# A graph network of four layers on one core: the tiles for further edges of the relation layer, one ahead of the other

## What is computed

```
agg  = segment_sum(x[src], edge_type * n + dst)          # 34 relations x 625 nodes
mean = agg / max(count, 1)
h1   = einsum('nri,rio->no', mean, W_rel) + x @ W_root + b_rgcn
```

## Time and profile before

| | |
|---|---|
| median of 3 runs | 2348.77 us (2345.55 to 2357.88) |
| the profiled execution's own time | 2364.8 us |
| its span | 2363.0 us |
| PE busy | 2022.8 us, 86% of the span |
| DVE, ACT, POOL busy | 52%, 35%, 25% |
| mean granted TensorE clock | 0.933 |
| relation stage with its root product | 987 to 1538 us |
| further tiles | 1538 to 1592 us |

### The profile page before, as it was taken

One profiled execution on the slowest core, in us unless ns is written; L12 is line 12 of the kernel. 1 busy time (PEld: TensorE's weight loads), 2 busy tenths in 40 slices (PEclk: granted clock), 3 DMA queues, 4 the chain that ended last, 5 costly groups with the idle time before them and its releaser, 6 DMA issues.

```text
span 2363.0 us, 33949 instructions
## 1 busy us (share of the span) xinstructions
PE 2022.8 (86%) x10920; PEld 1723.1 (73%) x10921; DVE 1218.2 (52%) x2168; ACT 830.6 (35%) x1050; POOL 596.0 (25%) x538
## 2 busy tenths in 40 slices
PE   3998998989999999689999999957778778678885
PEld 3988986758889967489999999944465656647663
DVE  5752224454443655755555555434543776646773
ACT  1222222321222223245445554433330356312763
POOL 0003756610000076434444442007710000000000
PEclk9999999999999999899999999978989889785998
DMA  3555668724445587548878878658820021110111
GB/s 110 159 156 157 176 173 288 248 97 148 151 151 165 159 286 236 171 157 258 265 250 266 262 249 271 219 196 270 269 81 7 14 66 31 40 32 29 56 45 39
DMA packets 203270, 378.38 MB, mean 160 GB/s; under 512 B 18810, under 2 KB 173626, under 8 KB 203176
## 3 DMA queue, kind: packets, MB, share of 16 engines
q1 hardware_dynamic: 170520, 246.23, 32.1%
q0 software_dynamic: 31216, 128.89, 18.0%
q10 hardware_dynamic: 1440, 1.97, 0.2%
HBM read 288.68 MB, written 88.34 MB: 160 GB/s over the span
## 4 chain that ended last, share of the span: by engine, by line
PE 35%; DVE 7%; DMA 5%; issue 5%; ACT 4%; POOL 2%; ACTq 0%; SPq 0%; DVEq 0%; another core or an unknown queue 0%; POOLq 0%
PE ps L1657 19%; PE ps L1855 5%; DMA arena<-in_L_gnn_W_rel 2%; PE ps L1820 2%; POOL arena L491 2%; PE ps L1783 1%; PE ps L1670 1%; PE ps L1891 1%; DMA arena<-U,ix 1%; ACT arena L762 1%; PE ps L1906 1%; PE ps L1489 1%; DVE arena L1302 1%; DVE al L1306 1%; PE ps L1807 1%
## 5 line engine op out<-in xcount | busy, mean ns | idle before, releaser
L1657 PE MATMUL ps<-w_hi,hT_hi 128*128 128x384 f32 x2052 | 722.3, 352 | 48.0 <-DVE hT_lo L1064 16.4
L1657 PE MATMUL ps<-w_lo,hT_hi 128*128 128x384 f32 x2052 | 696.8, 340 | 0.0
L1657 PE MATMUL ps<-w_hi,hT_lo 128*128 128x384 f32 x2052 | 696.6, 339 | 0.0
L1657 PEld LDWEIGHTS ps<-w_hi,hT_hi 128*128 128x128 f32 x2052 | 394.5, 192 | 60.9 <-issue 28.8
L491 POOL DMA_INDIRECT arena<-U,ix x252 | 272.7, 1082 | 495.6 <-DMA U<-arena 378.0
L1657 PEld LDWEIGHTS ps<-w_lo,hT_hi 128*128 128x128 f32 x2052 | 393.8, 192 | 0.1
L1657 PEld LDWEIGHTS ps<-w_hi,hT_lo 128*128 128x128 f32 x2052 | 393.0, 192 | 0.0
L1093 DVE TENSOR_TENSOR w_lo<-arena,w_hi 128x2304 fp32r<-128x2304 f32 x67 | 171.5, 2560 | 148.8 <-ACT w_hi L619 137.7
L571 ACT ACTIVATE arena<-ps 128x384 f32<-128x384 f32 x160 | 78.1, 491 | 482.6 <-PE ps L1657 431.4
L1568 PE MATMUL ps<-arena,onehot 128*128 128x512 f32 x504 | 194.6, 510 | 16.6 <-DMA arena<-U,ix 8.7
L527 POOL DMA_INDIRECT h<-h_d,lidx x68 | 117.5, 1728 | 292.1 <-PE ps L1670 250.2
(11 more groups left out here) (256 smaller groups left out, 2871.0 us busy)
## 6 DMA issues: line engine op xcount, KB each, us to landing
arena<-in_L_gnn_W_rel SPq DMA_DIRECT2D x74, 1152.0 KB, 5.6
U<-arena SPq DMA_DIRECT2D x292, 192.0 KB
arena<-in_L_gnn_W SPq DMA_DIRECT2D x36, 1152.0 KB
U<-z SPq DMA_DIRECT2D x28, 864.0 KB
arena<-rows_d SPq DMA_DIRECT2D x42, 320.0 KB, 3.5
arena<-in_L_gnn_root SPq DMA_DIRECT2D x4, 1152.0 KB
arena<-U,ix POOLq DMA_INDIRECT x252
arena<-in_L_gnn_W_root SPq DMA_DIRECT2D x2, 1152.0 KB
```

The costliest lines, as they stand in the source:

```text
L1657: ins = pe.matmul(acc, l, r[:, j, kt, :], start=(n == 0), stop=(n == 3 * KT - 1))
```

## The change

Four things are rearranged.

- **List ahead.** The list of tile c + 1 is made between the two products of tile c (`further_index(c + 1)`), its rows are gathered beside the second product, and its transposes stand behind that (`further_turned`). Rows go to a slot of their own, `h[:, 2 * TC, :]`, and products to PSUM banks 4 and 5.
- **Two weight buffers.** Tiles load alternately to `raw_v[0]`, which lies where the ring of the message stage will be, and `raw_v[1]`, the old `raw`. The loop's body is written out twice for the two, four passes to a block. The gather of a tile that doesn't exist is skipped with a branch.
- **First tile in the relation stage.** Its one-hot pieces, list and row gather stand at the start of that stage, its two weight loads go out there too, and its transposes and the split of its rows and first half stand inside the last relation.
- **The rest.** `counts_out(1)` stands two rounds earlier, and the last rounds of DVE's loop are written out. Some semaphores are shared to make room.

```diff
@@ SP, relation stage
+            sp.wait_ge(S["ov_ok"], 1)
+            n_ov = sp.value_load(ov[0:1, 0, NV:NV + 1], min_val=0, max_val=NV)
+            r_first = sp.value_load(ov[0:1, 0, 0:1], min_val=0, max_val=R1 - 1)
+            for j in range(2):
+                sp.dma_start(raw_v[0][:, j], rel(Wr, r_first, j)).then_inc(vw_in[0][j], 16)
             with sp.Fori(0, R1 - 1) as it:
                 for j in range(2):
                     load(it, Q_REL + 2 + j, rel(Wr, it + 1, j))
                     store_rel(it, j)
+            def further_w(c, k, q):
+                with sp.If(c + 1 < n_ov):
+                    r = sp.value_load(ov[0:1, 0, ds(c + 1, 1)], min_val=0, max_val=R1 - 1)
+                    for j in range(2):
+                        if k == 0:
+                            sp.wait_ge(S["w_lo"], Q_REL + 2 * R1 + 1 + j)
+                        sp.wait_ge(S["v_lo"], 2 * c + j + 1)
+                        sp.dma_start(raw_v[1 - k][:, j], rel(Wr, r, j)).then_inc(vw_in[1 - k][j], 16)
@@ POOL
+                if b == 0:
+                    pool.wait_ge(S["l_ix"], 2)
+                    pool.indirect_dma_start(out=h[:, 2 * TC, :], out_offset=None, in_=h_d,
+                                            in_offset=bass.IndirectOffsetOnAxis(ap=vidx[:], axis=0)).then_inc(S["v_in"], 16)
@@ ACT, end of the relation stage and a further tile
+                            else:
+                                further_part(0)
+                                act.wait_ge(S["steps"], S_REL + 4 * TC * it + TC * (2 * rr + j) + 10)
+                                further_hi(0, 0, 0)
@@
+                further_hi(0, 0, 1)
                 act.wait_ge(S["evac"], S_REL + 2 * TC * R1 + 2)
@@
                     for j in range(2):
                         act.wait_ge(S["v_mm"], 2 * c + j + 1)
                         act.wait_ge(v_st[j], 16 * c + 16)
-                        act.activation(ust[:, j, :], ps[:, j, 0:HALF], cp).then_inc(S["v_ev"], 1)
+                        act.activation(ust[:, j, :], ps[:, 4 + j, 0:HALF], cp).then_inc(S["v_ev"], 1)
+                        if j == 0:
+                            with act.If(c + 1 < n_ov):
+                                further_hi(1 - m, q + m, 0)
+                    with act.If(c + 1 < n_ov):
+                        further_part(c + 1)
+                        further_hi(1 - m, q + m, 1)
@@ DVE, start of the relation stage, and a further tile
                 split(0, o + 1)
                 further_list()
+                dve.wait_ge(S["ov_ok"], 1)
+                further_one_hot(0)
+                further_index(0)
                 bias(o, v, 0)
                 split(0, o + 2)
@@
+                def tile(c, m, q):
+                    further_index(c + 1)
+                    with dve.If(c + 1 < n_ov):
+                        further_lo(c + 1, 1 - m, 0)
+                        further_part(c + 1)
+                        further_one_hot(c + 2)
+                        further_lo(c + 1, 1 - m, 1)
@@ PE
                 for j in range(2):
                     for g in range(NG):
                         step(0, Q_L1 + j, g)
                 pe.wait_ge(S["l_ix"], 1)
+                further_index(0)
                 for i in range(3):
                     hc_part(0, 0, i)
+                pe.wait_ge(S["l_ix"], 2)
@@
+                                if last and rr == 1 and TC * j + g == TC - 1:
+                                    pe.wait_ge(S["acc_out"], 4)
+                                    further_turned(0)
@@
+                def tile(c, m, q):
                     pe.wait_ge(S["hc_lo"], 3 * R1 + 2 * c + 3)
                     for j in range(2):
+                        if j == 1:
+                            further_index(c + 1)
                         pe.wait_ge(S["v_lo"], 2 * c + j + 3)
-                        product(ps[:, j, 0:HALF], (hv_hi, hv_lo), j, slice(0, P)).then_inc(S["v_mm"], 1)
+                        product(ps[:, 4 + j, 0:HALF], (hv_hi, hv_lo), j, slice(0, P)).then_inc(S["v_mm"], 1)
+                    with pe.If(c + 1 < n_ov):
+                        further_turned(c + 1)
```

More of the change, by code:

```diff
@@ L221, in gnn_kernel @@
             "c_oh c_pe ct_tp ct_cp deg_ok deg_sq gcn_y gcn_mm gcn_ev x_ok ln_c ln_cc ct_ln cl_hi "
-            "elu_v elu_m elu_e bd_z bd_tp bd_ok ft_mm ft_ev chain out_st").split()}
+            "elu_v elu_m elu_e bd_tp bd_ok ft_mm ft_ev chain").split()}
         w_in = [sem("w_in0"), sem("w_in1")]
@@ L226, in gnn_kernel @@
         hc_in = [sem("hc_in0"), sem("hc_in1")]
-        vw_in = [sem("vw_in0"), sem("vw_in1")]
+        vw_in = [[sem(f"vw_in{k}{j}") for j in range(2)] for k in range(2)]
         v_st = [sem(f"v_st{j}") for j in range(2)]
@@ L282, in each_further @@
                 with eng.If(b * NVB < n_ov):
-                    with eng.Fori(0, NVB) as i:
-                        with eng.If(b * NVB + i < n_ov):
-                            steps(b * NVB + i)
+                    with eng.Fori(0, NVB // 2) as i:
+                        for k in range(2):
+                            c = b * NVB + i * 2 + k
+                            with eng.If(c < n_ov):
+                                steps(c, k, b * (NVB // 2) + i)
         def sums(c0, g=None):
@@ L540, in _, with further_rows @@
             n_ov = pool.value_load(ov[0:1, 0, NV:NV + 1], min_val=0, max_val=NV)
[L542 to L546, removed]
+            def further_rows(c, k, q):
+                with pool.If(c + 1 < n_ov):
+                    pool.wait_ge(S["l_ix"], c + 3)
+                    pool.sem_inc(S["pool_nop"], 1)
+                    pool.indirect_dma_start(out=h[:, 2 * TC, :], out_offset=None, in_=h_d,
+                                            in_offset=bass.IndirectOffsetOnAxis(ap=vidx[:], axis=0)).then_inc(S["v_in"], 16)
             each_further(pool, n_ov, further_rows)
+            pool.wait_ge(S["v_lo"], 4)
             for g in range(2 * TC):
@@ L1104, in relations @@
                 pair(lo, True)
-                with dve.Fori(lo + 1, R1 // 2 - 1) as it:
+                pair(lo + 1, False)
+                counts_out(1)
+                for it in range(lo + 2, R1 // 2 - 1):
                     pair(it, False)
                 pair(R1 // 2 - 1, False, True)
-                counts_out(1)
+                further_lo(0, 0, 1)
             def further():
                 n_ov = dve.value_load(ov[0:1, 0, NV:NV + 1], min_val=0, max_val=NV)
[L1113 to L1127, removed]
-                                                         hv_hi[:, 3 * i:3 * i + 3, :].bitcast(F32), ALU.max, ALU.subtract).then_inc(S["hc_lo"], 1)
+                def tile(c, m, q):
[5 more added lines that the diff above has]
+                        further_lo(c + 1, 1 - m, 1)
                 each_further(dve, n_ov, tile)
@@ L1221, in _ @@
             dve.sem_inc(S["v_lo"], 2)
[L1222 removed]
+            dve.wait_ge(S["x_dma"], 32)
             ln(0)
@@ L1659, in product, with further_index, further_turned @@
                 return ins
+            def further_index(c):
+                pe.wait_ge(S["l_oh"], R1 + c + 1)
+                for g in range(NG):
+                    ins = pe.matmul(ps[:, 6, CW:CW + 1], oh_v[:, g, :], nid[:, g:g + 1], start=(g == 0), stop=(g == NG - 1))
+                ins.then_inc(S["l_pe"], 1)
+            def further_turned(c):
+                pe.wait_ge(S["v_in"], 16 * c + 16)
+                pe.wait_ge(S["hc_lo"], 3 * R1 + 2 * c + 1)
+                for kt in range(KT):
+                    ins = pe.transpose(ps[:, 2 + kt // 3, P * (kt % 3):P * (kt % 3 + 1)], h[:, 2 * TC, P * kt:P * (kt + 1)], ident[:])
+                    if kt % 3 == 2:
+                        ins.then_inc(S["hc_tp"], 1)
             def relations(stride, side):
```

98 lines of the change are left out of this document (50 added, 48 removed).

## The result

The change takes 2338.45 us (median of 7 runs, 2333.11 to 2341.71) against 2351.18 us before (7 runs, 2339.88 to 2357.88). The ratio is 0.9949, with a 95% interval of 0.9929 to 0.9969: 12 us less, by the interval 7 to 17. The forecast was 10.6 us less.

A forecast was written before the change was run, and what follows sets the result against it. PE was taken to bound the relation stage, waits the further tiles. 15.9 us saved in the tiles, minus 4.1 (start), 0.7 (transposes) and 0.5 (stores), gave 10.6 less: median 2348.77 to 2338.2 us, range 2331 to 2346.

The forecast's parts named there:

- What bounds: Relation stage: PE busy 97.2 of 100 us, so its losses reach the end; further tiles: some 24 us are waits.
- The start: Relation stage's start: DVE waits for PE's list with bias and first `w_lo` queued behind; 4.1 us more, 3.6 to 4.7.
- Tile 0 and tile 1: First products start about 2 us and 16.6 us after E, the last relation's end; tile 0 before was at 12.7.
- ACT holds tile 1 back by 3: Before tile 1: its rows would allow E (last relation's end) + 13.6, but ACT's store wait and split delay it 3 us.
- The gather of 4.27 us: Row gather between two further tiles, priced at its length in the profile before, within the 8.4 us chain.
- Tile 2: Third further tile: begins 30.3 us after E, the last relation's end, from tile 1's first product of 5.3 plus 8.4.
- The 8.4 us from list to product: Between two further tiles: list, `vidx`, POOL, gather, transposes, splits, product; stays 8.4 us, second product beside the gather.
- The clock: Tile 2's first product: clock may hold over a 5 us gap; 4.3 us taken, the middle of 3.2 and 5.3.
- the rule that every tile starts at the lower clock: Trainium skill's rule for loops waiting on a DMA between bursts; tile 2 starting slowly would make the saving 1.0 us smaller.
- The sum: Whole kernel: 15.9 less in the further tiles, minus 4.1, 0.7 and 0.5, gives 10.6 us less.
- Transposes and `counts_out`: Six transposes in the last relation cost 0.7 us, at most 1.3; `counts_out` in DVE's 3.77 us gap costs nothing.
- The moved loads: Weight loads moved: nothing at the stage's start, bound 8.8 us; 0.5 at its end for later stores. Collision rival: chance 0.17.

The follow-up runs named there:

- e1: The change with DVE's wait for the first list put behind the first bias and `w_lo`; 2332.45 us, 0.9905 of the kernel before.
- e5: The change with the further tiles' products copied to a free part of `h`, so ACT doesn't wait for the last relation's stores; 2331.58 us, 0.9938 of before.
- e2: The change with one weight buffer in place of two, each later half loaded once the half before it is split; 2338.49 us, 0.9935 of before.
- e3: The change with the next tile's list behind both products, and DVE's `vidx` copy behind a split; 2347.84 us, 0.9973 of before.
- e6: The change with the edits of e1 and e5 together; 2330.44 us, 0.9918 of the kernel before.
- e7: e6 with matmuls of zeros on PE in the gaps between tiles; 2328.68 us, 0.9907 of the kernel before.
- e4: The change with the first tile's list, gather, transposes and splits behind the last relation again, weights still loaded early; 2341.46 us, 0.9942 of before.

## Why the prediction was right

**What bounds.** The reading held: PE in the relation stage, waits in the further tiles. That the start's 4.2 us went on to the end of the stage fits all profiles (no stage is shorter by as much after the change), but the scatter of the stage, 8 us in before alone, is too wide to show it by itself.

**The start.** Forecast 4.1 us more, measured 4.2. The place was named (DVE's wait for PE's list, with bias and `w_lo` behind it), and e1 shows that it is the whole of it.

**Tile 0 and tile 1.** Forecast E + 2 and E + 16.6; measured E + 2.3, and 16.7, 16.8 and 16.6 in three profiles. One step that is half wrong is inside: "the rows themselves would allow E + 13.6, so ACT holds tile 1 back by 3". e5 showed 15.2; ACT held it by 1.5. The gather of 4.27 us was priced from rows of before, where little else moved, and close behind a weight load it takes 5.5 to 6.5. The sum wasn't touched, since ACT was last. On ACT itself two terms were wrong and cancelled; they stand below, under the moved loads.

**Tile 2.** Forecast E + 30.3; measured 30.1, 29.4 and 30.4. The 8.4 us from list to product were 7.9, with transposes at the full clock, and the first product of tile 1 took 5.0 to 6.1 where 5.3 stood.

**The clock.** I took the middle of 3.2 and 5.3 us for tile 2's first product. The three profiles gave 5.8, 3.4 and 6.1: both levels, and more often the lower, so the rule that every tile starts at the lower clock held in two of three. A product of 18 takes 6.12 when the clock doesn't rise within it (granted clock 0.50 in tile 1 of the third profile), which rows 4 didn't show. Tile 0's first product, for which I took 3.2, also came at both: after a gap of 2.3 us its granted clock was 1.00, 0.65 and 0.67. The fast case isn't free either: in that profile the second product waited 0.9 us for `w_lo`. The last product ended at E + 39.3, 37.3 and 39.9 (forecast 38.1).

**The sum.** For E to the first gather the forecast was 15.4 less with the 0.5 for the stores; measured 15.9. For the whole 10.6 less was forecast. The two columns give 11.6, with the transposes 10.9, and the timed runs 12 with 5 to either side.

**Transposes and `counts_out`.** Six transposes took 0.66 us, as said. `counts_out` took 1.81 us in DVE's idle time and left 2.00 of it, in the change's timeline:

```profile
1484.08 1.81 DVE L1248 COPY counts<-ps 128x1600 f32<-128x1600 f32 x1
1487.90 2.56 DVE L1148 TENSOR_TENSOR w_lo<-arena,w_hi 128x2304 fp32r<-128x2304 f32 x1 [2.00 <-ACT w_hi L644]
```

**The moved loads.** That they collide with the stores at the end holds, and I had it too small. The last stores landed in 5.75 us against 3.52, 2.2 more, where I took 0.5, and the other profiles agree (5.6 and 5.8 in the change, 3.5 to 3.6 before). In e1, e2, e3, e5, e6 and e7, where a weight load goes out 0.9 us ahead of E as well, they landed in 5.4 to 5.7 us; in e4, where none does, in 2.14.

And yet tile 1 came when forecast, because another term was wrong the other way. I had put the four stores behind ACT's split of tile 0's second half, 2.13 us. In ACT's timeline of the change they go out while the split runs:

```profile
1540.05 2.12 ACT L619 ACTIVATE w_hi<-arena 128x2304 fp32r<-128x2304 f32 x1
1540.18 1.97 ACTq L664 DMA_DIRECT2D U<-arena  x4
```

The last of them is out at E + 1.96, exactly as in rows 3 (1539.56 against 1537.6). So the 2.13 us were not paid, and the 2.2 us of slower landing stood in their place: ACT's first split for tile 1 began at E + 10.96, where E + 10.6 was forecast.

At the start of the stage nothing shows a cost. The first tile's two loads went out at 1002.5 and 1003.1 and landed within 8.3 us, and the root product beside them took 43.8 to 45.3 us, against 41.6 to 45.2 before.

By the Trainium skill ("DMA: Bandwidth & Descriptors", "Issuing engines are not separate DMA queues") transfers of different engines share the same DMA engines and interleave. The traces agree: the row gather took 4.1 to 4.3 us for tile 2 of the change, with no weight load in the air, and 5.46, 6.27 and 6.51 when it went out 1.5 to 2.1 us behind one (e5, e7, e2); tile 1's gather in the first profile of the change, 1.5 us behind one, took 6.1. About 3 us behind one it took 4.2 to 5.0 (the other two profiles of the change, e1, e6).

**What was luck.** The base of the prediction was one profile above the median, slowest of four in three parts that the change doesn't touch. This did no harm because the sum was made within the two places. But inside the second place it was the fastest of the four: 60.7 us from E to the first gather against 62.2 to 62.9, since its pairs of products took 7.9 to 8.5 us and those of the others 8.8 to 9.2. Against its own base the change saves 14.5 us there and not 15.4; the means are 15.9 apart. That the two terms on ACT cancelled was luck too, and so was the median: 2338.2 was forecast and 2338.45 measured, while the median of before moved from 2348.8 to 2351.2. In the stated range the upper end doesn't follow from its own words (a gain of 5 and 9 us of spread would give 2353, not 2346); the result lies far from either end.

## What to carry to other kernels

When work of a later stage is put ahead in an earlier one, look on each engine at what is queued behind its new waits: here one line's place on DVE costs 4.2 us of a gain of 15.9, and it is had back for nothing by putting the wait behind what was ready. In a chain of list, gather, transposes and product, the second product belongs beside the gather, and in the one profile that tests it the second weight buffer pays by keeping a load out of the gather's time, not by making weights early. Ask of every transfer that is put earlier which small store or gather on the chain it will now run beside: a weight load 0.9 us ahead of E made the stores that ACT waits for land 3 us later than without it. Effects of 5 us in 2340 are read from the distance between two events in the trace, which repeats to within 0.5 us (2.2 where the clock comes in), and not from the span, which scatters by 20 us.

## What the runs showed that I had not expected

- Rests between events far from the change scatter by several us from one execution to the next, in both kernels: 968 to 979 us up to the store of `h`, 111 to 124 us for the same 84 gathers.
- The same tile in the same program starts at either clock: tile 2's first product took 5.76 us in one profile of the change, 3.40 and 6.12 in the others.
- The last relation's four stores landed in 2.14 (e4), 3.52 (before) and 5.75 us (the change) after the last of them was issued. Weight loads go out 5.1 and 4.4 us ahead of E in before (1532.5 and 1533.2), 0.9 ahead of it in the change, and only at E + 9.9 in e4.
